# An earlier second gate load, and 24 instead of 20 token tiles' gates on VectorE, in a graph-and-experts kernel

## The reference, cut

```python
x = x + gnn0(layernorm(x), adj, W0, b0)     # x: 4096 x 256, adj: 4096 x 4096 of 0 and 1
x = x + ffn0(layernorm(x))                  # 8 experts, each token goes to its best 2
x = x + gnn1(layernorm(x), adj, WL, bL)
x = x + ffn1(layernorm(x))                  # integer work on a few columns

def gnn0(h, adj, W, b):
    A = (adj != 0)
    return A @ (h @ W + b) / sum(A, axis=0)[:, None]

def ffn0(xt):
    logits = xt @ Wg + bg                   # 256 x 8
    ...                                     # softmax, top 2, gelu(xt @ W1 + b1) @ W2 + b2
```

## Time and profile before

| | us |
|---|---|
| median of 3 runs | 1022.38 (1021.75 to 1022.44) |
| the profiled execution, its time | 1022.8 |
| its span, from the first to the last instruction | 1021.0 |
| mean granted TensorE clock | 0.961 |
| TensorE matmuls busy | 929.0 (91%) |
| VectorE busy | 590.0 (58%) |
| ScalarE busy | 400.7 (39%) |
| GpSimd busy | 429.6 (42%) |

### The profile page before, as it was taken

The page is one execution under the profiler, slowest core; times in us unless marked ns, Lnnn a source line. Parts: engine busy times, 40 slices in busy tenths (PEclk is TensorE's granted clock), DMA queues, the critical chain, the costliest instruction groups (busy, mean ns, idle before and its releaser), DMA issues. The chain is left out here.

```text
span 1021.0 us, 21671 instructions
## 1 busy us (share of the span) xinstructions
PE 929.0 (91%) x6625; PEld 608.5 (60%) x6626; DVE 590.0 (58%) x1878; ACT 400.7 (39%) x837; POOL 429.6 (42%) x437
## 2 busy tenths in 40 slices
PE   8999899999913899999999999999379999999994
PEld 4354444444502799989989889899234454444442
DVE  6641996866698755655655655656256151251644
ACT  5858669576796443232232232233012101010111
POOL 3463746425576245545545545545444400210110
PEclk9999999999955999999999999999789999999997
DMA  9988899899786423323322332333299979775770
GB/s 324 411 290 312 317 335 351 289 337 382 249 284 182 160 45 48 54 46 47 54 45 47 53 47 46 53 47 46 44 336 402 370 230 327 266 263 166 242 259 26
DMA packets 91577, 199.92 MB, mean 196 GB/s; under 512 B 14241, under 2 KB 47266, under 8 KB 91394
## 3 DMA queue, kind: packets, MB, share of 16 engines
q1 hardware_dynamic: 74482, 168.37, 46.7%
q0 software_dynamic: 17040, 30.87, 14.8%
HBM read 177.05 MB, written 22.16 MB: 195 GB/s over the span
## 5 line engine op out<-in xcount | busy, mean ns | idle before, releaser
L1043 PE MATMUL bank<-adj_f,feat 128*128 128x512 f16 x1024 | 240.0, 389 | 5.2 <-DMA adj_f<-in_adjT 3.8
L1329 ACT ACTIVATE act_f<-bank,b_sb 128x256 f32<-128x256 f32 (+1 forms) x312 | 122.2, 449 | 255.4 <-PE bank L1260 255.4
L1260 PE MATMUL bank<-rT,experts 128*128 128x256 f16 (+1 forms) x1872 | 189.6, 262 | 2.5 <-DVE rT L1368 2.5
L1272 PE MATMUL bank<-experts,act_h 128*128 (+1 forms) x1680 | 189.1, 273 | 0.0
L1730 PE MATMUL bank<-adj_g,feat 128*128 128x512 f16 x768 | 179.7, 388 | 1.2 <-POOL feat L1556 1.2
L1260 PEld LDWEIGHTS bank<-rT,experts 128*128 (+1 forms) x1872 | 167.2, 98 | 19.8 <-DVE rT L1368 2.9
L1043 PEld LDWEIGHTS bank<-adj_f,feat 128*128 128x128 f16 x1024 | 97.1, 96 | 130.9 <-DMA adj_f<-in_adjT 6.0
L1272 PEld LDWEIGHTS bank<-experts,act_h 128*128 128x128 f16 x1680 | 163.0, 98 | 18.2
L925 ACT ACTIVATE spent<-adj_f 128x1024 f16<-128x1024 f32 x128 | 135.1, 1055 | 32.3 <-DMA adj_f<-in_adjT 27.1
L1187 POOL DMA_INDIRECT x_rows<-y,token x70 | 115.8, 1655 | 67.9 <-issue 58.2
L1730 PEld LDWEIGHTS bank<-adj_g,feat 128*128 128x128 f16 x768 | 74.4, 97 | 94.5 <-issue 2.1
(11 more groups left out here) (274 smaller groups left out, 978.5 us busy)
## 6 DMA issues: line engine op xcount, KB each, us to landing
adj_f<-in_adjT SPq DMA_DIRECT2D x128, 512.0 KB, 7.0
adj_g<-in_adjT SPq DMA_DIRECT2D x72, 512.0 KB, 6.0
adj_early<-in_adjT SPq DMA_DIRECT2D x24, 512.0 KB, 7.3
adj_g<-in_adjT SPq DMA_DIRECT2D x48, 256.0 KB, 3.1
unit_f<-in_W SPq DMA_DIRECT2D x16, 512.0 KB, 7.2
stage<-in_W SPq DMA_DIRECT2D x12, 512.0 KB, 6.5
x_ring<-in_x POOLq DMA_DIRECT2D x16, 256.0 KB, 7.1
x_rows<-agg SPq DMA_DIRECT2D x4, 1024.0 KB, 8.9
```

Of the source, the lines that this page charges most:

```text
L1043: last = pe.matmul(mine(s)[ib * DC + c][:, :], feat0[:, j, h, c * P:(c + 1) * P], adj_0[j % RING][:, ib * HALF_SWEEP:(ib + 1) * HALF_SWEEP ...
L1260: last = pe.matmul(pb[2 + q][:, k * SLOT + at:k * SLOT + at + width], w1_part(mine_e * DC + (f // FQ * W2_UNIT0 + c), wh)[:, (f % FQ) * P: ...
L1272: last = pe.matmul(pb[6 + r][:, 0:D], act_h[:, ah, f, r * P:(r + 1) * P], experts[:, ds(e[r] * DC + (W2_UNIT0 + f // UH), 1), wh, (f % UH) ...
L1329: last = a.activation(act_f[q][:, k, at:at + width], pb[2 + q][:, k * SLOT + at:k * SLOT + at + width], ACT.Gelu, bias=b1_sb[:, ds(mine_e ...
```

## The change

Four edits. The two loads of the gate weights stand next to each other in GpSimd's queue, ahead of the split of W1 unit 2 (the wait for the first turn stays between them). XT_TILES is 8: TensorE transposes and multiplies 8 token tiles in sweep 0, and VectorE makes the gates of 24. These are spread as 9 tiles (72 products) in sweep 1, 11 (88) in sweep 2 and 4 (32) at the start of sweep 3; before, they were 8, 10 and 2. split_w0g moves behind take_x_gates in VectorE's queue.

```diff
-    XT_FROM, XT_EACH, XT_TILES = 22, 2, 12
+    XT_FROM, XT_EACH, XT_TILES = 22, 2, 8
...
             load_gate_rows(0)
-            split_unit(2)
             pool.wait_ge(sem("wg_half_turned"), 1)
             load_gate_rows(1)
-            for u in range(3, W2_UNIT0):
+            for u in range(2, W2_UNIT0):
                 split_unit(u)
...
             for n in range(XT_TILES):
                 take_transposed(n)
-                if n == 9:
-                    split_w0g()
             take_x_gates()
+            split_w0g()
             split_w0()
...
-            for s, ahead, behind in ((1, 0, 6 * E), (2, 4 * E, 4 * E)):
+            for s, ahead, behind in ((1, 0, 7 * E), (2, 4 * E, 5 * E)):
```

## The result

The changed kernel takes a median of 1014.51 us (four runs, 1014.01 to 1015.04) beside 1022.41 us of the kernel before (four runs, 1021.75 to 1023.65): a ratio of 0.9921 [0.9905, 0.9937], so 0.8% faster, with an interval that excludes no change. I had predicted 1016.1 us, in 1014.8 to 1019.6. The sign is right; the gain is 7.9 us where the sum said 6.25, and the median lies 0.3 us under the range. Repeated later beside each other, the kernel before stood at 1.0003 [0.9994, 1.0012] and the changed one at 0.9929 [0.9914, 0.9944], 7.3 us faster, with a median of 1015.21 in five runs (1012.51 to 1016.53). That median lies inside the range, so by how much the first one missed it is partly chance. Three later runs that took far longer than the others of the same kernel (1168.26 us of the changed one, 1248.18 and 3431.14 of the one before) are left out of all medians and ratios.

The account below looks back on a forecast made before the run. The prediction took TensorE to set the pace, with a stall in sweep 1. The stall's 4.95 us and four tiles' 1.30 us sum to 6.25 us, taken off the median of 1022.38: 1016.1 us, range 1014.8 to 1019.6.

Parts of the forecast that it names:

- the sum: 4.95 us for the stall in sweep 1 plus 1.30 us for four tiles in sweep 0: 6.25 us less.
- The chain that makes the stall: Sweep 1: unit 2's high half, its split, the second gate load, the turn, the rows, then TensorE, idle 3.18 us.
- 4.95 us for the stall: Sweep 1, row behind tile 12: 3.33 us lost, plus 1.62 us more partly at the slower clock.
- 1.30 us for four tiles: Sweep 0: four transposed tiles fewer on TensorE, 0.325 us each, straight on the path.
- Products on VectorE cost nothing on the path: Sweeps 1 to 3: 32 more products on VectorE, costed at nothing; between nothing and 3.5 us.
- The feed in sweep 1 costs nothing: Tile loads behind unit 9's load in sweep 1: no stall expected, 1.5 us if that load's issue did not move.
- Sweeps 2 and 3 and all behind them shift as they are: Everything behind sweep 1 was to come earlier with unchanged length, adding nothing to the 6.25 us.
- the two terms: The 4.95 us for the stall in sweep 1 and the 1.30 us for four tiles in sweep 0.
- Rival 1: Sweep 1: the feed takes the stall's place, giving back 1.5 or 3.1 us: 1017.6 to 1019.2; chance 0.15.
- rival 3: Sweep 1: the stall is not removed and only the 1.30 us stay: 1021.1 us; chance 0.08.
- Rival 2: Sweep 3: VectorE's lateness reaches the path, giving back up to 3.5 us: 1017 to 1019.6; chance 0.11.
- Rival 4: Sweep 3, row 20: slower, TensorE waits from 8.4 us of VectorE lateness; 15 us gives 1024.4 and up; chance 0.06.

Follow-up runs that it names:

- e3_loads_only: The kernel before with only the order of the two gate loads and W1 unit 2 changed, 12 tiles staying on TensorE: 1017.69 us, ratio 0.9957.
- e4_tiles_only: The kernel before with all edits but the load order, so 8 tiles on TensorE and unit 2 between the gate loads: 1019.58 us, ratio 0.9970.
- e13_split_later: The kernel before with only split_w0g moved behind take_x_gates on VectorE: 1022.29 us, ratio 0.9999.
- e12_before_pad32: The kernel before with 32 more matmuls, whose results nobody reads, at the end of TensorE's program: 1020.70 us, ratio 0.9981.
- e7_late32: The changed kernel with 32 products repeated on VectorE at the start of sweep 3: 1024.23 us, ratio 1.0019 against the kernel before.
- e11_ten_tiles: The changed kernel with 10 tiles on TensorE and 22 on VectorE: 1014.7 us in a single run.
- e14_after_pad64: The changed kernel with 64 more matmuls, whose results nobody reads, at the end of TensorE's program: 1013.81 us in a single run.
- e5_six_tiles: The changed kernel with 6 tiles on TensorE and 26 on VectorE: 1016.33 us, ratio 0.9939 against the kernel before.

## Why the prediction was off by 1.6 us, step by step

- **The chain that makes the stall**: right. The load order alone removes it (e3_loads_only), the other edits don't (e4_tiles_only). Predicted second issue at 82.3 to 84.5, measured 81.94, a little early as all of sweep 0 was; second turn at 88.0 to 92.4, measured 89.36; VectorE free at 92 to 97, measured 93.26.
- **4.95 us for the stall**: right, 4.97, as it was priced from rows of the very program that was changed. Its second half, the fall of the clock, is less fixed than its first: in e13_split_later TensorE idles the same 3.18 us, but sweep 1 takes 69.40 us, 1.2 more than before, with a granted clock of 0.50 in the 4.8 us behind the idle time where the earlier trace rows had 0.64.
- **1.30 us for four tiles**: right, 1.31, and 0.33 a tile at every size tried.
- **Products on VectorE cost nothing on the path**: right. The sum of the low half in sweep 1 stands 2.8 us late (141.60 against 138.21 + 0.63, the distance it has in sweep 2) and nobody waits; I had said 0 to 3. In sweep 2 the idle time shrank from 4.77 to 1.78, by 2.99, near the 2.8 of the free pitch. In sweep 3 the 32 products start from 204.49 to 215.21, 0.346 apart. The root wait became 4.17 (I had said about 4.5). The last root, though, was not late by 2 us: its wait fell to 0.29, and the sums behind it wait the same 2.74 for TensorE. By the Trainium skill ("SBUF — State Buffer", "Who interferes with whom") a VectorE instruction with two SBUF inputs and a GpSimd instruction that reads SBUF contend. The trace agrees on both sides: in sweep 3, with GpSimd idle from 204 to 216 us, the products start 0.346 us apart, and in sweep 1 one of 2.34 us at 102.60 stands behind GpSimd's tensor-tensor of 2.41 at 102.25.
- **The feed in sweep 1 costs nothing**: right, for the reason given. Unit 9's load is issued at 123.00, 7.07 us earlier than in the earlier trace rows, while the sweep's end moved by 7.66 (145.87 to 138.21): it moves nearly as much as TensorE does, and TensorE is busy 63.30 of 63.30 us.
- **The step that failed: "Sweeps 2 and 3 and all behind them shift as they are", and with it the unspoken one that all ahead of tile 22 stays as it is.** The sweeps did (63.25 each). The first 54 us and the stretch behind the sweeps did not: 1.38 and 0.5 us of the profiled 8.2, and some 1.0 to 1.6 us of the medians (7.3 and 7.9 less the 6.28 of the two terms). The sum put both at nothing without a reason. Of the 1.38 us, 1.25 are shorter waits for the first adjacency tiles and an earlier first tile; what made these shorter is open. The comparison of e12_before_pad32 with the kernel before shows that an edit which leaves all work as it is can go with a median 1.8 us lower. I had given the low side of the range 1.3 us under the sum, for "a little more than the sum", where one such shift needs two.
- **Rivals.** Rival 1 (feed) and rival 3 (stall stays) are refuted by the windows of sweep 1. Rival 2 did not come: at 3.1 us of lateness nothing waits. Rival 4's place holds, its price does not: at 14.2 us of lateness e7_late32 shows 6.29 us of wait at row 20, and by the rule this lateness costs 5.8 + 1.6 = 7.4 us, while the profile shows 10.3 (9.15 in sweep 3, 1.18 behind it). That its 1024.23 us lie so near the 1024.4 that I had put at 15 us is luck: the gain that I had left out makes up for part of the price. Its "it decides from 8.4 us on" also missed ScalarE's nearer margin, which at 8.7 us already costs 4.4.

**What stays open.** Why the landings differ, and why the clock fell at the start in four profiles of kernels with twelve tiles and in none with fewer. The two groups of W0 marks do not overlap, six profiles against eight, which speaks against chance alone; but three profiles of each group are of one program, and ten and six tiles and the padding don't fall in line with any property that I varied. The DMA engines are as good as full where it happens, so that a small shift in their order could make a tile land 1 to 3 us later; that is argued, and what would shift it wasn't found. The placement of the program or of its tensors in memory would be a candidate; this wasn't tried. Of all versions none is shown to beat the changed kernel: e11_ten_tiles (1014.7) and e14_after_pad64 (1013.81) are single runs within its spread.

## What to carry to other kernels

In this kernel a stall whose chain was followed to its first cause could be priced to a few hundredths of a microsecond, its idle time and the slower clock behind it apart, and so could work that leaves an engine which is busy throughout. Around such a sum I would now leave some 2 us of 1000 on both sides: a stretch that waited for full DMA engines moved by over 1 us with nothing changed in it, and work added behind the end went with a median 1.8 us lower. To tell such a shift from a gain, cut the span at marks that both kernels share, look at the granted clock and the waits of each stretch, and pad a kernel with work whose results nobody reads before explaining the last 0.2%.

## What the runs showed of the hardware that I had not expected

- The same work with 32 more matmuls behind its end ran at 0.9981 [0.9969, 0.9993] of its time; the cause is open.
- The clock fell behind a wait of 1.97 us in e12_before_pad32, where one of 0.93 us had ended 5.8 us earlier: the 16 matmuls behind it took 5.39 us instead of 3.79. Behind a wait of 2.34 us in e5_six_tiles it did not (16 in 3.78). The length of the last wait alone did not tell what the clock would do. TensorE's timeline, first of e12_before_pad32:

```profile
29.04 5.39 PE L1043 MATMUL bank<-adj_f,feat 128*128 128x512 f16 x16 [1.97 <-DMA adj_f<-in_adjT]
```

then of e5_six_tiles:

```profile
24.59 3.78 PE L1041 MATMUL bank<-adj_f,feat 128*128 128x512 f16 x16 [2.34 <-DMA adj_f<-in_adjT]
```

- The same idle time of TensorE (3.18 us) cost 1.62 us of slower clock behind it in one program and 2.8 in another: the row behind the stalled one came after 4.72 us and the next after 3.06, where the earlier trace rows had 4.11 and 2.49. TensorE's timeline in e13_split_later:

```profile
106.48 0.40 PE L198 MATMUL bank<-w0s,sum_hi 128*128 128x266 f16 x1 [3.18 <-DVE agg L588]
...
111.20 0.42 PE L198 MATMUL bank<-w0s,sum_hi 128*128 128x266 f16 x1
...
114.26 0.27 PE L198 MATMUL bank<-w0s,sum_hi 128*128 128x266 f16 x1
```

and the window behind the idle time, in which TensorE ran at 1.2 GHz throughout (0.50):

```profile
106.50:111.30 4.80, 4.80 (x15) 2.13 (x16) 4.80 (x23) 4.18 (x8) 1.95 (x2) 0.50 0.99 397
```
